# A softmax in quarters of the rows, another order at the scan's end, and network rows handed over in halves

## The reference

```python
# 1: keep the rows with the largest norm, as many as a gate on cond says
rows_to_keep = clip(int(sigmoid(cond @ score_w + score_b) * 1024), 1)
y = x * (norm(x, axis=-1) >= sorted_norms[rows_to_keep - 1])[..., None]
# ... a Mamba block on y
xz = rmsnorm(y, rms_w) @ in_proj;  xi, z = split(xz)           # 512 channels each
xi = silu(causal_conv(xi, 4 taps) + conv_b)
dt, Bm, Cm = split(xi @ x_proj, [16, 32]);  delta = softplus(dt @ dt_w + dt_b)
h = exp(delta * A) * h + (delta * xi) * Bm;  ys = sum(h * Cm)   # 16 states, scan over 1024 rows
x = x + y + ((ys + xi * D) * silu(z)) @ out_proj
# 2: attention in which every query of a batch and head is the same vector
q, k, v = x @ Wq.T, x @ Wk.T, x @ Wv.T                          # 16 heads of 16
qmod = sum_s((t @ Wt.T . q_s) * q_s)                            # one per batch and head
attn = softmax(where(mask, qmod . k / 4, -max)) ;  o = (attn @ v) @ Wo.T
# 3: a network 256 -> 1024 -> 1024 -> 1024 -> 256 on o
h = silu(o w1 * s1) * (o w2 * s2);  h = gelu(h h1 * s3);  h = gelu(h h2 * s4)
x = x + h w3 * s5
```

## Time and profile before

| | us |
|---|---|
| median of 3 runs | 551.34 |
| the profiled execution | 554.95 |
| its span | 553.2 |
| PE busy | 467.1 |
| DVE busy | 458.3 |
| ACT busy | 383.4 |
| POOL busy | 379.6 |

### The profile page before, as it was taken

One profiled execution on the slowest core, in us unless ns is written; L12 is line 12 of the kernel. 1 busy time (PEld: TensorE's weight loads), 2 busy tenths in 40 slices (PEclk: granted clock), 3 DMA queues, 4 the chain that ended last, 5 costly groups with the idle time before them and its releaser, 6 DMA issues.

```text
span 553.2 us, 7943 instructions
## 1 busy us (share of the span) xinstructions
PE 467.1 (84%) x2773; PEld 336.6 (61%) x2773; DVE 458.3 (83%) x532; ACT 383.4 (69%) x671; POOL 379.6 (69%) x230
## 2 busy tenths in 40 slices
PE   8967898769858998898789998886897949989992
PEld 6423765446547665765676557555896738877651
DVE  4869899998999799779997997899999988961422
ACT  3675687679977787868877978798768768831210
POOL 5029868866999688839995897599979967610001
PEclk9987899977999999889999999899999977998997
DMA  9331011111102111110021011100210590029004
GB/s 289 122 118 39 39 39 39 38 43 38 31 25 98 39 40 38 41 38 1 40 77 39 38 40 41 39 18 25 74 39 38 172 398 13 1 66 380 1 1 156
DMA packets 18207, 39.40 MB, mean 71 GB/s; under 512 B 1697, under 2 KB 10529, under 8 KB 18162
## 3 DMA queue, kind: packets, MB, share of 16 engines
q1 hardware_dynamic: 18162, 38.84, 20.1%
HBM read 36.61 MB, written 2.23 MB: 70 GB/s over the span
## 4 chain that ended last, share of the span: by engine, by line
PE 42%; DVE 30%; issue 14%; ACT 10%; POOL 3%; DVEq 0%; POOLq 0%; ACTq 0%
DVE scanmem L1860 18%; PE hT L931 8%; DVE yTd L1871 6%; PE pp L576 5%; PE pp L669 4%; PE yacc L640 3%; PE dA L893 2%; ACT dA L1378 2%; PE pp L618 2%; POOL scanmem L1535 2%; PE pp L791 2%; PE yacc L636 1%; DVE yTd L1785 1%; PE pp L632 1%; PE pp L864 1%
## 5 line engine op out<-in xcount | busy, mean ns | idle before, releaser
L1535 POOL TENSOR_TENSOR scanmem<-par,scanmem 128x1024 f32<-128x1024 f32 x128 | 300.5, 2372 | 82.4 <-PE hT L931 63.0
L931 PE MATMUL hT<-con,scanmem 128*128 128x128 f32 x1024 | 163.1, 290 | 59.2 <-DVE yTd L1871 43.1
L1378 ACT ACTIVATE dA<-par,Aneg 128x512 f32<-128x512 f32 x256 | 171.9, 690 | 47.1 <-DVE scanmem L1860 45.7
L931 PEld LDWEIGHTS hT<-con,scanmem 128*128 128x128 f32 x1024 | 120.4, 147 | 114.6 <-DVE yTd L1871 39.6
L1860 DVE TENSOR_TENSOR_SCAN scanmem<-dA,carry,scanmem 128x512 f32<-128x512 f32 x128 | 156.3, 1263 | 11.4 <-ACT dA L1378 10.4
L1860 DVE TENSOR_TENSOR_SCAN scanmem<-dA,scanmem 128x512 f32<-128x512 f32 x128 | 148.8, 1204 | 10.2 <-ACT dA L1378 8.4
L1388 ACT ACTIVATE hc<-hT,CTs 128x512 f32<-128x512 f32 x128 | 86.8, 678 | 30.9 <-PE hT L931 30.7
L640 PE MATMUL yacc<-con,hc 128*128 128x128 f32 x512 | 83.1, 288 | 0.0
L1871 DVE SCALAR_TENSOR_TENSOR yTd<-hT,CTs,yTd 128x512 f32<-128x512 f32 x91 | 66.1, 726 | 9.4 <-PE hT L931 9.2
L640 PEld LDWEIGHTS yacc<-con,hc 128*128 128x128 f32 x512 | 65.8, 151 | 0.0
L576 PE MATMUL pp<-xnT,wi 128*128 128x512 f32 x120 | 58.9, 619 | 2.6 <-DVE par L1659 1.3
(11 more groups left out here) (210 smaller groups left out, 530.7 us busy)
## 6 DMA issues: line engine op xcount, KB each, us to landing
scanmem<-brow SPq DMA_DIRECT2D x32, 512.0 KB, 3.7
par<-in SPq DMA_DIRECT2D x1, 4096.0 KB, 17.7
scanmem<-in SPq DMA_DIRECT2D x1, 4096.0 KB, 13.6
xt<-in SPq DMA_DIRECT2D x4, 512.0 KB, 6.7
wi<-in SPq DMA_DIRECT2D x2, 1024.0 KB, 8.0
out<-par SPq DMA_DIRECT2D x3, 512.0 KB, 4.4
aw<-in SPq DMA_DIRECT2D x5, 256.0 KB, 6.5
xr<-in SPq DMA_DIRECT2D x1, 1024.0 KB, 10.2
```

Of the source, the lines that this page charges most:

```text
L931: last = nc.tensor.transpose(hT[:, i % 2, m * P:(m + 1) * P], hb[:, n % RING, m, i * P:(i + 1) * P], ident)
L1378: A(dA[:, m % 2, :], delta(c)[:, m, :], ACT.Exp, scale=Aneg[:, m * NS + s:m * NS + s + 1]).then_inc(da_ready, 1)
L1535: nc.gpsimd.tensor_tensor(hb[:, n % RING, ms, :], dx(c)[:, ms, :], Bb[:, row:row + 1, :].to_broadcast([P, 2, T]), ALU.mult).then_inc(bx_re ...
```

## The change

1. The scores of batch and head are laid out by quarters: each of the four groups of 32 rows of the bank gets its own 256 of the 1024 rows, in four small products that take different columns of the array (job `S`). The scores are computed negated, so the minimum is taken. Each quarter is exponentiated against its own minimum; a transpose of the minima (job `MT`) gives every row the minimum over the four quarters, ACT makes the quarter's weight from it (`quarter_weight`), and job `LT` sums the weighted sums.
2. The scan's last step transposes tiles 0 and 1 group by group as the scans end, and tiles 2 and 3 into the banks of the factors. The skip products of tiles 1 and 3 move before the transposes of step 62. DVE gates tile 0 before it gathers tile 3. The last output products are four jobs of one tile each, and the tail has another order.
3. Network rows are scaled in two halves, with a semaphore after the first.
4. `kept` and the new small steps use SCALAR_TENSOR_TENSOR.
5. The mask of the scores is loaded in four pieces of 256 columns; attention of batch 0 has 15 places in place of 14.

```diff
-ATT = [7, 8, 8, 10, 12, 14, 15, 16, 18, 21, 23, 24, 25, 28]
-ATT1 = [28, 29]
+ATT = [7, 8, 8, 10, 12, 14, 15, 16, 18, 20, 22, 23, 25, 26, 28]
+ATT1 = [24, 27]
...
-    tail += [("Y", last, 1), ("Y", last, 3), ("O", last, 0), ("AP", 1, 0), ("O", last, 1), ("AT", 1, 0), ("G", 1, 1), ("R", last, 0), ("GT", 1, 0),
-             ("M", 1, 0), ("R", last, 1)]
+    tail += [("Y", last, 1), ("Y", last, 3), ("O", last, 0), ("AP", 1, 0), ("O", last, 2), ("AT", 1, 0), ("O", last, 1), ("O", last, 3),
+             ("R", last, 0), ("G", 1, 1), ("R", last, 1), ("GT", 1, 0), ("M", 1, 0)]
...
-WARM = {**{(name, 1, 0): 2 for name in ("GT", "RR", "PT", "YV", "YT", "VV", "WO")}, ("AT", 1, 0): 4,
-        ("S1", 1, 0): 10, ("W12", 0, 0): 3, ("WT", 0, 0): 3, ("H", 1, 0): 3, ("HT", 1, 0): 1,
+WARM = {**{(name, 1, 0): 2 for name in ("GT", "RR", "PT", "YV", "YT", "VV", "WO")},
+        ("S", 1, 0): 3, ("MT", 1, 0): 2, ("W12", 0, 0): 3, ("WT", 0, 0): 3, ("H", 1, 0): 3, ("HT", 1, 0): 1,
...
+            def job_S(job, o):
...
                 for k in range(KD):
-                    last = mm(o, r_sb[:, k, :, :], x1T[:, k, j * 512:(j + 1) * 512], start=k == 0, stop=k == KD - 1)
+                    for q in range(NQ):
+                        last = mm(o[q * QR:(q + 1) * QR, 0:QT], r_sb[:, k, :], x1T[:, k, q * QT:(q + 1) * QT], start=k == 0, stop=k == KD - 1, tile_position=(0, q * QR))
...
+            def job_MT(job, o):
+
+                wait_read(pe, ("S", job[1], 0))
+                return nc.tensor.transpose(o[:, 0:P], st_neg.to_broadcast([P, P]), ident)
...
+            def job_LT(job, o):
+
+                pe.wait_ge(share_ready, job[1] + 1)
+                return mm(o[:, 0:1], sel_same, st_share, start=True, stop=True)
...
+            def last_transposes(i, ms):
+
+                n = NCH * NS - 1
+                if i == 0:
+                    pe.wait_ge(mul_done, 2 * n)
+                if i == 1:
+                    pe.wait_ge(pool_mul_done, pool_sums(n - 1))
+                for m in ms:
+                    pe.wait_ge(scan_done, CT * n + m + 1)
+                    last = nc.tensor.transpose(turned_bank(n, i)[:, m * P:(m + 1) * P], hb[:, n % RING, m, i * P:(i + 1) * P], ident)
+                if ms[-1] == CT - 1:
+                    last.then_inc(hT_ready, 1)
...
             def softmax(b):
-                act.wait_ge(mx_ready, b + 1)
-                for h, total in ((0, 2), (1, 5)):
-                    half = sm[:, h * 512:(h + 1) * 512]
-                    A(half, half, ACT.Exp, bias=st[:, 1:2], accum_out=st[:, total:total + 1]).then_inc(p_ready, 1)
+                wait_read(act, ("S", b, 0))
+                A(p_q, p_q, ACT.Exp, bias=st_neg, scale=-1.0, accum_out=st_sum).then_inc(p_ready, 1)
+
+            def quarter_weight(b):
+                wait_read(act, ("MT", b, 0))
+                A(st_w, st_neg, ACT.Exp, bias=st_top, scale=-1.0).then_inc(w_ready, 1)
...
-            def softmax(b):
-                wait_read(dve, ("S1", b, 0))
-                V.tensor_scalar(st[:, 1:2], st[:, 0:1], -1.0, None, ALU.mult).then_inc(mx_ready, 1)
-                dve.wait_ge(p_ready, 2 * (b + 1))
-                own.mark(V.tensor_tensor(st[:, 2:3], st[:, 2:3], st[:, 5:6], ALU.add))
-                own.after()
-                V.reciprocal(st[:, 3:4], st[:, 2:3]).then_inc(recip_ready, 1)
...
+            def ev_LT(job, o):
+                return V.reciprocal(st_recip, o[:, 0:1])
+
+            def after_job(job):
+                name, b, _ = job
+                if name == "PT":
+                    dve.wait_ge(p_ready, b + 1)
+                    dve.wait_ge(w_ready, b + 1)
+                    V.scalar_tensor_tensor(st_share, st_sum, 1.0, st_w, ALU.mult, ALU.mult).then_inc(share_ready, 1)
+                    if b == 1:
+                        compare_rows()
+                if name == "LT":
+                    wait_read(dve, job)
+                    V.scalar_tensor_tensor(st_c, st_recip, 1.0, st_w, ALU.mult, ALU.mult).then_inc(recip_ready, 1)
...
+            def scaled_row(o, scale):
+
+                V.tensor_tensor(row[:, 0:256], o[:, 0:256], scale[:, 0:256], ALU.mult).then_inc(half_row, 1)
+                return V.tensor_tensor(row[:, 256:512], o[:, 256:512], scale[:, 256:512], ALU.mult)
...
-                if job[0] == "S1":
-                    softmax(job[1])
-                    if job[1] == 1:
-                        compare_rows()
+                after_job(job)
...
-                own.mark(V.tensor_scalar(keep[:, gs], cnt[:, gs], 1.0, fr[:, 2, b:b + 1], ALU.add, ALU.is_le))
+                n = gs.stop - gs.start
+                own.mark(V.scalar_tensor_tensor(keep[:, gs], cnt[:, gs], 1.0, fr[:, 2, b:b + 1].to_broadcast([P, n]), ALU.add, ALU.is_le))
                 own.after()
-                V.tensor_scalar(keep1[:, gs], keep[:, gs], 1.0, None, ALU.add).then_inc(ranked, 1)
-                V.tensor_tensor(scl[:, gs], keep[:, gs], lnv[:, gs], ALU.mult).then_inc(scl_ready, 1)
+                V.scalar_tensor_tensor(keep1[:, gs], keep[:, gs], 1.0, keep[:, gs], ALU.add, ALU.max).then_inc(ranked, 1)
+                V.scalar_tensor_tensor(scl[:, gs], keep[:, gs], 1.0, lnv[:, gs], ALU.mult, ALU.mult).then_inc(scl_ready, 1)
...
             mac_step(n - 1, 1)
+            gate_even(NCH - 1, 0)
             mac_step(n - 1, 3)
-            gate_even(NCH - 1, 0)
             gate_even(NCH - 1, 2)
```

More of the change, by code:

```diff
@@ L28 @@
 NQ = P // QR
-NSEL = NH + 2 * NQ + 2 * B + B
+NSEL = P + 2 * NQ + 2 * B + B
+QT = S // NQ
 XW = DR + 1 + 2 * NS
@@ L337, in build @@
         gf3 = small[:, 1, DM:2 * DM].rearrange("p (k t) -> p k t", k=KD)
+        p_q, others = sm[:, 0:QT], sm[:, 2 * QT:2 * QT + P]
+        st_neg, st_sum, st_top, st_w, st_share, st_recip, st_c = (st[:, i:i + 1] for i in range(7))
         g_row, y_row = sm[:, 0:DM], sm[:, DM:2 * DM]
@@ L767, in job_G @@
                     wait_read(pe, ("AT", 1, 0))
-                    wait_read(pe, ("O", NCH - 1, 1))
+                    for i in range(NT):
+                        wait_read(pe, ("O", NCH - 1, i))
                 else:
@@ L949, in reduce, with last_skip @@
                 last.then_inc(red_done, 1)
+            def last_skip(i):
+                job = ("Y", NCH - 1, i)
+                wait_free(job)
+                for m in range(CT):
+                    skip(bank(job), NCH - 1, i, m, m == 0)
+            def last_transposes(i, ms):
[9 more added lines that the diff above has]
+                    last.then_inc(hT_ready, 1)
             def squares_turned(b, dst):
@@ L1679, in ev_O @@
                 _, e, j = job
-                for i in range(2):
+                for i in range(1 if e == NCH - 1 else 2):
                     g = e * NT + j + 2 * i
```

144 lines of the change are left out of this document (78 added, 66 removed).

## The result

The changed kernel takes 559.31 us at the median of 4 runs (557.47 to 559.68). The ratio to the kernel before, of comparable runs on the same chip, is 1.0097, 95% interval 1.0051 to 1.0144. A second comparison with more runs (12 against 35) gave 559.58 against 556.85 us, ratio 1.0084 (1.0054 to 1.0115). A ratio compares only those executions of each kernel that lie within 1.5% of its fastest, so it can differ from the ratio of two medians. The change is within 2%, but it is slower by some 3 to 5 us. The forecast was 2.1 us faster, range 543.5 to 558: wrong in sign, and the measured time is 1.3 us outside the range.

A forecast was written before the change was run, and what follows sets the result against it. DVE paces the 64-step scan, about 5.6 us a step, then a serial end of some 60 us; no engine is full. 2.9 + 0 + 0.1 + 2.25 - 3.5 + 0.4 = 2.15 us gained: 551.34 to 549.2 us, range 543.5 to 558.

The forecast's parts named there:

- Part 1: Softmax of batch 0 inside the scan: 26.2 us becomes 20.8 + X, a gain of 2.9 us.
- the addition: DVE's one-element sum in batch 0's old softmax, 3.43 us, ending 0.02 us behind POOL's product.
- X: Cost of the two new one-element multiplications in batch 0's softmax, taken as 2.5 us, between 0.3 and 8.7.
- rival 2: Three-operand forms are held until POOL pauses, as the addition was: 554 to 559 us, chance 0.25.
- Rival 1: Three-operand forms are not held by POOL: X = 0.3, part 2 gains 1.2, 545.8 us; chance 0.18.
- Part 2: Row counts of batch 1 with three-operand forms: held as now, taken as 0; smaller mask step 0.2, longer constants 0.1 against.
- Part 3: End of the scan: first output product at 492.4 for 494.03, projection 2.1 us and scores 2.6 us earlier.
- Part 4: Softmax at the end: value rows copied 2.25 us earlier, comparison waiting for the mask; 3.5 us lost to PE's low clock.
- The stall: PE idle from about 511.9 to 517.3 before the value rows' copy, then at half clock: 3.5 us lost.
- Rivals 3 and 4: PE's clock holds at the end: alone 545.7 us, chance 0.12; with rival 1 542.3 us, chance 0.05.
- Part 5: Network rows in halves: three handovers, at most 0.2 us each, 0.4 us gained (0 to 0.6).
- the differences carry over: Gain reckoned on the profiled 554.95 us execution was applied unchanged to the median of 551.34 us.

The follow-up runs named there:

- e11_act_pad: e2_split with the second new one-element multiplication on ACT and 13 idle products at the end of PE's program; 548.03 us, ratio 0.9883 to the kernel before.
- e10_no_quarters: Changed kernel with the old softmax, constants, mask load and `ATT1`, comparison behind the reciprocal; 560.00 us, ratio 1.0103 to the kernel before.
- e5_old_end: e2_split with the scan's end as in the kernel before, including four idle products behind AT; 553.43 us, ratio 0.9968 to the kernel before.
- e4_again: Changed kernel once more, nothing edited; 559.58 us, ratio 1.0084 to the kernel before.
- e12_mask_first: Changed kernel with the mask issued ahead of the 4 MB of weights and the comparison behind job M's read; 553.01 us, ratio 0.9960 to the kernel before.
- e2_split: Changed kernel with the mask comparison cut in two, behind the reads of `VV` and `WT`; 552.39 us, ratio 0.9929 to the kernel before.
- e3_warm: Changed kernel with 15 idle products in place of 2 behind the weighted value rows, job YV; 555.46 us, ratio 1.0006 to the kernel before.

## Why the prediction was wrong

**Part 1, the largest error on the average: the old softmax was priced from one execution, and the steps behind it were left out.** The 26.2 us from the first score read to step 60 hold the addition's 3.43 us, which is not a constant of the kernel: four more traces with the old softmax have 1.14, 0.50, 3.41 and 1.14. The same stretch takes 23.8 us in the mean of these five and 21.4 in the mean of the ten traces with both new multiplications on DVE: 2.4 us gained, near to the forecast 2.9. (In the profiled pair it is 26.2 and 21.8. That 26.2 is 9.8 us above three steps is a slip; it is 9.4, and the sum doesn't use it.) But 2.0 us of that are lost again in steps 60 to 63, where the forecast had nothing. Most of it is step 61, which takes 5.79 us in all five old traces and 6.8 to 7.9 in the ten; DVE's scan waits for ACT's factor there. In the changed kernel:

```profile
475.51 2.46 DVE L1921 TENSOR_TENSOR_SCAN scanmem<-dA,carry,scanmem 128x512 f32<-128x512 f32 x2 [2.01 <-ACT dA L1428]
```

The clock is at 0.50 from 472.1 us on here, but e11_act_pad, at full clock, still has 6.9 us. The change had moved the places of the attention jobs in these steps (`ATT`, and `ATT1` from 28 and 29 to 24 and 27). e10_no_quarters, with the old places and the old softmax, has 5.79 us, e5_old_end, with the old end of the scan, 7.91; no run undoes only the places, so whether they or the quarters cost it stays open. Together the last eight steps took 54.4, 50.6, 50.0, 54.4 and 50.6 us with the old softmax, mean 52.0, and 50.4 to 55.8 in the ten, mean 51.6. So the quarters with their places gave 0.4 us there on the average, with a spread of 5, not 2.9. Steps 56 to 63 of the profiled pair differ by 2.5 us and so seemed to confirm it; the repetition of both kernels shows no gain (50.6 and 50.6).

**X was right in the profiled execution by luck and is not a number.** Both multiplications together took 2.3 us in four of the ten traces, 0.3 in five and 5.8 in one. The five are no case of a multiplication that passes beside a busy POOL: the second fell into a pause of POOL, which waited 0.8 us for PE's transposes, with PE's clock at 0.50. In e4_again:

```profile
461.20 0.16 DVE L1776 SCALAR_TENSOR_TENSOR st<-st 128x1 f32<-128x1 f32 x1
461.73 2.37 POOL L1586 TENSOR_TENSOR scanmem<-par,scanmem 128x1024 f32<-128x1024 f32 x1 [0.81 <-PE hT L960]
```

In the four with 2.3 us the clock was at 1.00 at this place and POOL went on. What sets where the low stretches lie, no run shows. The rule of the Trainium skill, page "SBUF — State Buffer", section "Who interferes with whom", that the second to start waits until the first finishes, holds for rows of 2.17, 1.14 and 0.50 us, which end at the first end of a POOL instruction; three rows (3.43, 3.41, 5.62) waited on over one or two further ends, as rival 2 had it. Rival 1's 545.8 and rival 2's 554 to 559 were both priced as lasting states of the kernel; they are draws of one execution.

**Part 2 was right**: 1.99 and 1.19 us; 0.

**Part 3 was too large, but the sum used it only through the mask's issue.** From the end of the scan the first output product came 0.75 us earlier (5.05 for 5.80), not 1.6; the scores 0.8 to 1.3 and not 2.6. The forecast times were right to 0.1 to 0.7 us on the clock of the trace (first output product 491.73 for 492.4, copy 517.00 for 516.95), but only by luck: both had been worked out with the scan's end left at 488.2 and the scan's gain stands in the sum beside them, so with 2.9 us of it the copy was forecast for 514.05. The scan had ended 1.56 us earlier in that trace, and the stretch behind it was longer than forecast.

**Part 4: the mechanism was right, the sizes short.** Reckoned from the scan's end the copy came 0.65 us earlier and not 2.25: the mask landed 16.9 us after its issue and not 15.5 (15.5 to 16.5 in five traces with the old softmax, 15.1 to 17.9 in the others but e12_mask_first, so 15.5 was a short draw), and it was issued 0.2 us later behind the scan's end. The stall took 4.0 us in place of 3.5. Rivals 3 and 4 (the clock holds) did not occur in any of three traces with the stall: copy to gated layer 10.6 to 11.3 us. What the 3.5 was set against was again a good execution, though: in the kernels without the stall this stretch takes 6.7 us in five traces and 8.2 to 9.4 in eight. Against the mean of these the stall costs nearer to 3 us. The cause of the loss was stated in the forecast itself: without the comparison the copy would come at about 511.5 and not at 516.95, 5.4 us, and the 3.5 us of low clock would go too. e2_split is worth 7.2 us.

**Part 5 was right**: 0.52 us for 0.4.

**Not in the sum at all**: 1.3 to 2.1 us around the span and 1.0 us in the last transfers. The first was taken as constant with "the differences carry over"; the second comes of a longer constant tile and three more transfers at the program's start. Of these only the tile had a price, 57 KB of reading, 0.1 us.

**The start of the sum was low**: 551.34 us was the median of three runs, and the kernel before took 554.97 to 556.85 at the median of four later comparisons. The differences did not carry over from the profiled 554.95 us.

The sum of the profiled pair, from the traces: scan and what is ahead of it 1.56 gained, to the copy 0.65 gained, to the gated layer 3.98 lost, halves 0.52 gained, last transfers 1.05 lost, around the span 1.86 lost. That is 4.2 us lost; measured 4.06. Against the forecast of 2.15 gained, the scan is off by 1.4 us, the copy by 1.6, the stall by 0.5, the last transfers by 1.0 and the time around by 1.9. The 10.1 us between 549.2 and 559.31 are these 6.2, 3.6 of the low start, and 0.3 between the changed kernel's profiled execution and its median.

## What to carry to other kernels

A row that waits for another engine, and a stretch at low clock, must be priced from more than one execution: their length in one trace is a draw. Work on no path belongs into the wait that no one shares, and the place decides: the same 4.6 us of comparison cost 7 us more ahead of the reciprocal, and 2 us more behind it, than cut in two in two waits. A stretch must be priced to where the two kernels run alike again: here 2.0 of the 2.4 us were lost just behind the stretch that had been summed. A forecast made of parts is checked part by part from one origin of time; on the trace's clock two misses can look like a hit. A longer tile moves all tiles allocated behind it, and transfers into them can slow.

## What the runs showed of the hardware

- One-element DVE rows with two inputs in SBUF that started inside a POOL instruction were held for 0.50 to 5.62 us in all, TENSOR_TENSOR (to 3.43) and SCALAR_TENSOR_TENSOR (to 5.62) alike, and each ended within 0.03 us of the end of a POOL instruction. Those of 0.13 to 0.16 us fell on the last 0.07 us of one or into a pause of POOL. An ACT row on the same elements took 0.30 us beside the same stream.
- The granted clock fell to 0.50 behind PE stalls of 3.70 to 4.81 us (in each of three traces) and of 1.95 us, and in some executions without a stall (e12_mask_first, 6.8 us long); that the shorter stall was the cause is not shown. The same chunk of the scan, with no edit in it, took 117.9 us in one execution and 123.8 in another; its windows in e2_split and in e3_warm:

```profile
117.00:141.00 24.00, 20.81 (x88) 14.16 (x88) 20.52 (x23) 21.05 (x37) 16.21 (x9) 0.74 0.13 45
```

```profile
117.00:141.00 24.00, 21.66 (x71) 14.00 (x72) 18.79 (x21) 16.38 (x30) 12.80 (x6) 0.52 0.13 45
```

- Output transfers ran at 377 to 383 GB/s from tiles in the old place, at 336 to 345 from tiles 448 bytes further (twelve kernels), at 380 to 386 from tiles 512 bytes further.
- Time around the span is 1.8 us, 2.1 to 2.2 or 3.0 to 4.2 by the program; 8 PE rows behind its end were enough to change it.
